# Attention block of a gated cross-attention layer: products with V in two groups of eight heads instead of four groups of four

## What is computed

```
q, k, v = projections of layernorm(x), ctx, ctx;  per head h of 16 (D = 16)
attn = q k^T / sqrt(D)                     # [256, 256] per head
p    = softmax(attn)
out  = p v                                 # [256, 16] per head
x    = x + tanh(g) * (concat(out) Wo + bo)
```

## Time and profile before

| | us |
|---|---|
| median of 3 runs | 318.63 (318.26 to 318.68) |
| span of the profiled execution, first to last instruction | 315.9 |
| projections and what comes ahead of step 0 | 0 to 81 |
| attention steps 0 to 7 and their tail | 81 to 231 |
| feed-forward layer | 231 to 316 |
| PE busy over the span | 239.1 (76%) |
| DVE busy | 218.9 (69%) |
| ACT busy | 176.1 (56%) |

### The profile page before, as it was taken

The page is one execution under the profiler, slowest core; times in us unless marked ns, Lnnn a source line. Parts: engine busy times, 40 slices in busy tenths (PEclk is TensorE's granted clock), DMA queues, the critical chain, the costliest instruction groups (busy, mean ns, idle before and its releaser), DMA issues.

```text
span 315.9 us, 6549 instructions
## 1 busy us (share of the span) xinstructions
PE 239.1 (76%) x1781; PEld 159.2 (50%) x1785; DVE 218.9 (69%) x465; ACT 176.1 (56%) x327; POOL 124.5 (39%) x213
## 2 busy tenths in 40 slices
PE   1799897999543999999999999999610578823951
PEld 1678676777322575757565656556400233312630
DVE  2579787765611769696979798894144389975992
ACT  2327583666711676676767667678501478836920
POOL 3366655232113135353434444353022395410074
PEclk9999999999955999999999999999875599995895
DMA  7767999933303353535353544000000000000025
GB/s 240 192 163 238 340 259 258 233 101 102 100 0 84 75 116 80 112 84 115 73 115 70 117 81 101 1 1 2 3 3 0 0 2 0 0 0 0 3 95 172
DMA packets 29734, 29.45 MB, mean 93 GB/s; under 512 B 5136, under 2 KB 26384, under 8 KB 29712
## 3 DMA queue, kind: packets, MB, share of 16 engines
q1 hardware_dynamic: 26832, 27.87, 34.8%
q10 hardware_dynamic: 2880, 1.31, 1.6%
HBM read 20.65 MB, written 8.39 MB: 92 GB/s over the span
## 4 chain that ended last, share of the span: by engine, by line
PE 27%; issue 14%; DVE 13%; POOL 6%; ACT 5%; DVEq 1%; DMA 1%; POOLq 0%; ACTq 0%; SPq 0%
PE bank_o L1281 6%; PE bank_a L1264 6%; PE bank_m L1307 5%; PE bank_b L1251 5%; DVE neg_max L801 3%; POOL x_rows L562 2%; PE bank_m L1289 2%; POOL arena L541 2%; PE bank_m L1297 2%; DVE x_rows L900 1%; ACT wgu_rows L761 1%; POOL big L553 1%; DVE arena L1076 1%; ACT big L662 1%; DVE stats L908 1%
## 5 line engine op out<-in xcount | busy, mean ns | idle before, releaser
L801 DVE TENSOR_REDUCE neg_max<-bank_b 128x2 f32<-128x512 f32 x112 | 73.9, 679 | 24.3 <-PE bank_b L1251 24.3
L662 ACT ACTIVATE big<-bank_a 128x512 f32<-128x512 f32 x128 | 69.8, 589 | 27.3 <-PE bank_a L1264 26.8
L1264 PE MATMUL bank_a<-big 98*128 98x256 bf16 x256 | 49.9, 278 | 9.5 <-DMA big<-max_parts 7.9
L1251 PE MATMUL bank_b<-big 96*128 96x256 bf16 x224 | 43.8, 277 | 0.0
L1281 PE MATMUL bank_o<-big,v_cur 128*32 128x256 f32 x512 | 35.8, 399 | 4.5 <-POOL v_cur L470 3.6
L1264 PEld LDWEIGHTS bank_a<-big 98*128 98x128 bf16 x256 | 21.4, 98 | 20.6 <-DMA big<-max_parts 8.4
L1173 PE MATMUL bank_a<-arena,w_t 128*128 128x256 f32 x128 | 31.1, 393 | 0.5 <-DVE resid L812 0.5
L476 POOL CAST max_parts<-max_f 8x256 bf16<-8x256 f32 x16 | 6.5, 405 | 56.0 <-ACT max_f L620 50.3
L1414 PE MATMUL bank_b<-wd_t,arena 128*128 128x256 bf16 x96 | 16.1, 323 | 14.4 <-DVE arena L1082 14.2
L1173 PEld LDWEIGHTS bank_a<-arena,w_t 128*128 128x128 f32 x128 | 24.4, 198 | 4.2 <-DVE resid L812 1.0
L449 POOL TENSOR_TENSOR arena<-resid,arena 128x512 bf16<-128x512 f32 x16 | 18.4, 1159 | 18.3 <-ACT arena L601 18.3
(11 more groups left out here) (157 smaller groups left out, 473.0 us busy)
## 6 DMA issues: line engine op xcount, KB each, us to landing
qk_parts<-arena SPq DMA_DIRECT2D x8, 768.0 KB, 5.0
big<-qk_parts SPq DMA_DIRECT2D x32, 192.0 KB, 3.7
big<-qk_parts SPq DMA_DIRECT2D x32, 128.0 KB, 4.0
x_rows<-in_x SPq DMA_DIRECT2D x8, 256.0 KB, 5.4
big<-qk_parts SPq DMA_DIRECT2D x32, 64.0 KB, 4.0
out<-x_rows SPq DMA_DIRECT2D x8, 256.0 KB, 2.2
big<-in_ctx SPq DMA_DIRECT2D x7, 256.0 KB, 6.9
wd_rows<-in_L_ffn_w_down SPq DMA_DIRECT2D x1, 704.0 KB, 8.2
```

The source lines that it names most:

```text
L662: act.activation(p_buf[:, h % HH], bank_a[:, h % 2].rearrange("p (c s) -> p c s", c=QC), ACT.Exp, scale=SCALE).then_inc(exp_done, 1)
L801: dve.tensor_reduce(neg_max[:, p, :, h], bank.rearrange("p (c s) -> p c s", c=QC), axis=AX.X, op=ALU.max, negate=True).then_inc(max_done, 1)
L1251: done = mm(to, q_st[0:KR, p, h, c * P:(c + 1) * P], k_st[0:KR, p, h], start=True, stop=not masked)
L1264: done = mm(to, k_st[0:KM, p, h, k * P:(k + 1) * P], q_st[0:KM, p, h], start=True, stop=not masked)
```

## The change

The heads are taken in two groups of eight (`GH = 8`, `GROUPS = 2`). `pv` of a group is 16 matmuls that fill the whole of `bank_o`; `ot` copies 512 columns; `back` is four transposes into all of `bank_m`; `rec` and `div` take eight heads at once. `p_buf` no longer wraps: the probabilities of heads 8 to 11 go to `resid`, 12 to 15 to a free part of `arena`, so that all 16 are kept. `o_t` is one buffer of 512 columns instead of two of 256. The three tables are new.

```diff
-    GROUPS = H // 4
+    GH = 8
+    GROUPS = H // GH
...
-    PE_AT = {("pv", 3): H + 1, "max_tr": 1, ("back", 3): H + 3, ("pv", 0): 5, "att_tr": H + 5, "out": H + 7,
-             ("pv", 1): 9, "next_max_tr": 9, ("back", 0): 11, ("pv", 2): 13, ("back", 1): 13, ("back", 2): H}
+    PE_AT = {("pv", 1): H + 1, "max_tr": 1, ("back", 1): H + 3, "att_tr": H + 6, "out": H + 8, ("pv", 0): 9,
+             "next_max_tr": 10, ("back", 0): 12}
...
+        p_last = part(4 * QC * S).rearrange("p (h c s) -> p h c s", h=4, c=QC)
+        p_third = resid[:].rearrange("p a w n -> p (a w n)").rearrange("p (h c s) -> p h c s", h=4, c=QC)
+        def p_of(h):
+            return p_buf[:, h] if h < HH else p_third[:, h - HH] if h < HH + 4 else p_last[:, h - HH - 4]
...
-                if not (start and h < HH):
-                    act.wait_ge(pv_done, GROUPS * b + h // 4 - 1)
+                if not start:
+                    act.wait_ge(pv_done, GROUPS * (b - 1) + h // GH + 1)
+                elif h == HH:
+                    act.wait_ge(lo_done, 2 * B)
...
-                    act.wait_ge(ot_tr, GROUPS * b + g - 1)
-                act.activation(o_t[:, g % 2], bank_o[:, 0:S], ACT.Copy).then_inc(ot_done, 1)
+                    act.wait_ge(ot_tr, GROUPS * b + g)
+                act.activation(o_t, bank_o[:], ACT.Copy).then_inc(ot_done, 1)
...
-                    pe.wait_ge(exp_done, H * b + 4 * g + 4)
+                    pe.wait_ge(exp_done, H * b + GH * (g + 1))
...
-                    for k in range(QC):
-                        for n in range(4):
-                            h = 4 * g + n
-                            done = mm(bank_o[n * 2 * D:(n + 1) * 2 * D, 0:S], v_cur[:, p, k, h],
-                                      p_buf[:, h % HH, k], start=(k == 0), stop=(k == QC - 1))
+                    for q in range(2):
+                        for k in range(QC):
+                            for n in range(4):
+                                h = GH * g + 4 * q + n
+                                done = mm(bank_o[n * 2 * D:(n + 1) * 2 * D, q * S:(q + 1) * S], v_cur[:, p, k, h],
+                                          p_of(h)[:, k], start=(k == 0), stop=(k == QC - 1))
...
-                        done = tr(bank_m[:, c * P:(c + 1) * P], o_t[:, g % 2, c * P:(c + 1) * P], ident_f[:])
+                        for q in range(2):
+                            done = tr(bank_m[:, (2 * c + q) * P:(2 * c + q + 1) * P],
+                                      o_t[:, q * S + c * P:q * S + (c + 1) * P], ident_f[:])
```

More of the change, by code:

```diff
@@ L90, in flamingo_block @@
     CT = CW // P
-    PE_AT = {("pv", 3): H + 1, "max_tr": 1, ("back", 3): H + 3, ("pv", 0): 5, "att_tr": H + 5, "out": H + 7,
-             ("pv", 1): 9, "next_max_tr": 9, ("back", 0): 11, ("pv", 2): 13, ("back", 1): 13, ("back", 2): H}
-    DVE_AT = {("rec", 0): 12, ("div", 0): 13, ("rec", 1): 14, ("div", 1): 14, ("rec", 2): H, ("div", 2): H + 1,
-              ("div", 3): H + 5, ("rec", 3): H + 4, "residual": H + 8, ("stats", 0): H + 10, ("stats", 1): H + 11,
-              "means": H + 12, "row_max": H + 15}
-    ACT_AT = {("ot", 3): H + 1, "max": 1, ("ot", 0): 7, "att": H + 5, ("ot", 1): 11, "next_max": 9, ("ot", 2): 13}
+    PE_AT = {("pv", 1): H + 1, "max_tr": 1, ("back", 1): H + 3, "att_tr": H + 6, "out": H + 8, ("pv", 0): 9,
+             "next_max_tr": 10, ("back", 0): 12}
+    DVE_AT = {("rec", 1): H + 4, ("div", 1): H + 5, "residual": H + 9, ("stats", 0): H + 11, ("stats", 1): H + 12,
+              "means": H + 13, ("rec", 0): 13, ("div", 0): 14, "row_max": H + 15}
+    ACT_AT = {("ot", 1): H + 1, "max": 1, "att": H + 6, "next_max": 10, ("ot", 0): 10}
     POOL_CHUNKS, DVE_CHUNKS = (1, 4), (0, 2, 3, 5)
@@ L147, in flamingo_block @@
         max_parts = sb("max_parts", [HH, 2, 2, S], BF16)
-        rec = sb("rec", [P, 2, QC, 4])
+        rec = sb("rec", [P, GROUPS, QC, GH])
         stats1 = sb("stats1", [P, 2, QC, 6])
@@ L200, in flamingo_block @@
         resid = sb("resid", [P, 2, 2, EC * S])
-        o_t = part(2 * S, True).rearrange("p (a s) -> p a s", a=2)
+        o_t = part(2 * S, True)
         att = part(2 * QC * E).rearrange("p (a c e) -> p a c e", a=2, c=QC)
@@ L659, in exp @@
                 act.wait_ge(s_done, H * b + h + 1)
-                if not (start and h < HH):
-                    act.wait_ge(pv_done, GROUPS * b + h // 4 - 1)
-                act.activation(p_buf[:, h % HH], bank_a[:, h % 2].rearrange("p (c s) -> p c s", c=QC), ACT.Exp,
+                if not start:
+                    act.wait_ge(pv_done, GROUPS * (b - 1) + h // GH + 1)
+                elif h == HH:
+                    act.wait_ge(lo_done, 2 * B)
+                act.activation(p_of(h), bank_a[:, h % 2].rearrange("p (c s) -> p c s", c=QC), ACT.Exp,
                                scale=SCALE).then_inc(exp_done, 1)
@@ L701, in other @@
                 else:
-                    ot_copy(b, what[1], start and what[1] < 2)
+                    ot_copy(b, what[1], start and what[1] == 0)
             def step(b, p, i=None, first=False, ahead=True):
@@ L716, in _ @@
                 other(what, 7)
-                if what == ("ot", 3):
+                if what == ("ot", 1):
                     ffn_weights(8)
@@ L878, in _ @@
             project(7, 1, 3, xs=False, st=False, heads=range(12, 16))
-            rows = bank_m[:, 0:QC * P].rearrange("p (c h x) -> p c h x", c=QC, h=4)
+            rows = bank_m[:].rearrange("p (c h x) -> p c h x", c=QC, h=GH)
             def reciprocals(b, g):
                 dve.wait_ge(ot_tr, GROUPS * b + g + 1)
-                chain.then(dve.reciprocal(rec[:, g % 2], rows[:, :, :, D]))
+                chain.then(dve.reciprocal(rec[:, g], rows[:, :, :, D]))
             def divide(b, p, g):
                 chain.wait()
-                dve.tensor_tensor(att[:, p, :, 4 * D * g:4 * D * (g + 1)].rearrange("p c (h d) -> p c h d", h=4),
+                dve.tensor_tensor(att[:, p, :, GH * D * g:GH * D * (g + 1)].rearrange("p c (h d) -> p c h d", h=GH),
                                   rows[:, :, :, 0:D],
-                                  rec[:, g % 2].unsqueeze(3).to_broadcast([P, QC, 4, D]), ALU.mult
+                                  rec[:, g].unsqueeze(3).to_broadcast([P, QC, GH, D]), ALU.mult
                                   ).then_inc(nrm_done, 1)
@@ L975, in _ @@
             with dve.Fori(0, 3) as i:
-                chain.loop(i, 12)
+                chain.loop(i, 8)
                 step(i * 2 + 1, 1)
@@ L1352, in attend @@
                     used = other(what, 7, 1, used)
-                    if what == ("back", 3):
+                    if what == ("back", 1):
                         ffn_weights(8)
```

## The result

| | before | after |
|---|---|---|
| median of the runs, us | 318.63 (5 runs, 318.26 to 318.90) | 331.17 (5 runs, 329.49 to 335.59) |
| the profiled execution, us | (no time of its own) | 334.24 |
| its span, us | 315.9 | 332.3 |

The changed kernel is slower: ratio 1.040, 95% interval 1.033 to 1.047. The profiled execution of after is a long one; three others have spans of 327.4, 327.8 and 329.1. So the profiles differ by 16.4 and the medians by 12.5. The ratios of the experiments are to executions of before made beside them, with medians of 317.60 to 317.75.

A forecast was written before the change was run, and what follows sets the result against it. PE sets the period, and the change spends the relays' margins, so PE waits for maxima at heads 0 and 8. Terms 2.9 + 8.7 + 0.5 + 3.1 + 1.6 = 16.8 lift the span to 332.7, time 335.4 us, range 323 to 343.

The forecast's parts named there:

- The relay: From next_max_tr through ACT's copy, POOL, SP and two DMAs to head 0's scores: 4.72 us, binding after the change.
- margin at head 0: In the kernel before, the first relay is through 0.5 us before head 0 starts.
- The waits: PE waits for the relays in each loop step: 1.19 us at head 0 and 0.64 at head 8.
- The step: One loop step, between scores that follow out: 17.94 us against 16.20, +8.7 over five periods.
- the second relay: From max_tr to head 8's scores: before 1.9 us to spare, after through at 15.62, a 0.64 wait.
- Step 0 and its start: First attention step, up to zero of step 1: 119.85 instead of 116.98, +2.9 us.
- the stream up to there is the same: Step 0's reason for pricing the second half of pv 0 at 1.00, after a first half of 1.80 at low clock.
- The last step: Final attention step: starts +0.5 us later, then +3.1 up to the second weights piece behind pv 0.
- The tail: End after the last pv: the wider last group costs +1.6 us in pv, ot, back, rec and div.
- Relay hidden: Rival: the relay doesn't bind, step 16.1, time 321 us (319 to 325); chance 0.12.
- Fewer instructions pay: Rival: PE waits for DVE to free bank_m, so 0.66 a step of rec and div is saved; 315.6 us, chance 0.10.
- The clock falls: Rival: the wait at head 0 lowers PE's clock in each of six steps, 9.4 us more, 345; chance 0.08.

The follow-up runs named there:

- e4: Kernel before plus an idle POOL memset of 8 x 1024 ahead of each cast of maxima; 319.65 us, 1.006 of before.
- e3: Changed kernel, own tables, with SP issuing the first row's DMA right behind POOL's cast instead of after the subtraction; 323.48 us, 1.016 of before.
- e8: Changed kernel with DVE's rounding of feed-forward weights moved from the last step to head 8 of step 0; 332.96 us, 1.044 of before.
- e5: Kernel before with the feed-forward weights rounded in step 0 instead of the last step; 317.72 us, 1.000 of before.
- e6: Kernel before with weights rounded in step 0 and the first row's DMA issued early; 317.32 us, 0.998 of before.
- e9: Changed kernel with e1, e2 and e3 together, weights rounded in step 0, and stats and means earlier on DVE; 322.19 us, 1.014 of before.
- e11: e9 with the rounding of the weights left in the last step; 322.98 us, 1.017 of before.
- e13: e11 with next_max_tr, pv 0, back 0 and the ACT copies for them one head later; 317.86 us, 1.001 of before.
- e1: Changed kernel with next_max_tr ahead of pv 0, both behind head 10; 326.50 us, 1.028 of before.
- e2: e1 plus ACT's copy of the maxima taken ahead of ot 1; 325.36 us, 1.022 of before.

## Why the prediction came out, point by point

The forecast, 335.4 with 323 to 343, was 4.2 above the median, and 1.2 above the profiled execution against which the sum was made. Its cause was right: the relay binds, at the two places named. Its terms were less good than their sum. Between the profiles the forecast has 2.9 + 8.7 + 0.5 + 3.1 + 1.6 = 16.8 and the measurement 6.2 + 6.3 + 3.9 + 0.1 = 16.4, the last step being 3.9 against 3.6. That these sums agree to 0.4 is luck: step 0 and the last step were forecast 3.6 too cheap, the loop and the tail 3.9 too dear.

**The relay**, predicted as 0.50 + 0.54 + 1.16 + 2.52 = 4.72, is 0.50 + 0.56 + 1.14 + 2.49 = 4.69. The waits, predicted as 1.19 and 0.64, are 1.27 (from 129.42, when in a full stream head 0 would follow the pair of head 15) and 0.62; the idle times in brackets, 1.11 and 0.46, count from the end of the matmuls ahead. The relay and its margin at head 0 were rightly read from the kernel before: e4 shows the margin there, and e3 that after has none.

**The step**, predicted as 17.94, is 17.37 to 17.59, 17.45 on the mean; the term that failed is the price of `pv`. A group of four was taken as 1.00 (16 products, in the chain of before too), so eight as 2.00; 32 products take 1.86 there. Twice a step that is 0.28. Another 0.13 is in the second relay (4.81 from `max_tr` to head 8 against 4.94) and 0.14 in `out`, for which the earlier trace rows gave 1.88 and whose scores follow at 1.73. Together that is a step of 17.4, which three of the five are; the other two are about 0.2 longer, and why isn't settled. Five periods cost 6.3 instead of 8.7.

**Step 0 and its start**, predicted as +2.9, came to +6.2 (123.16 against 116.98), for three reasons, none of them in the sum: 1.0, 0.85 and 1.9, of which smaller terms give 0.4 back. Head 8 of step 0 started 1.0 later. The whole of `pv 0`, not half of it, ran at the low clock:

```profile
100.86 0.61 PE L1272 MATMUL bank_a<-big 98*128 98x256 bf16 x2 [13.20 <-DMA big<-max_parts]
...
102.68 3.60 PE L1290 MATMUL bank_o<-big,v_cur 128*32 128x256 f32 x32
```

against 2.75 predicted. The step that failed is the one from "the stream up to there is the same" to a second half at full clock. Three windows from the scores of head 8 to the end of the low clock, in before, after and e4 (groups of four):

```profile
99.83:103.17 3.34, 3.34 (x24) 1.61 (x24) 1.39 (x2) 1.20 (x2) 0.00 (x0) 0.50 1.03 220
100.86:106.10 5.24, 5.24 (x40) 2.43 (x40) 1.39 (x2) 1.19 (x2) 0.00 (x0) 0.50 0.70 149
99.82:105.40 5.58, 5.58 (x34) 2.92 (x35) 1.80 (x3) 2.16 (x4) 0.75 (x1) 0.50 0.68 140
```

The wait ahead was 7.9, 13.2 and 8.5, so its length alone doesn't decide how long the low clock lasts: e4, with the stream of before, has it as long as after. Before's 3.3 is the shortest of all fourteen profiles, and the forecast took it as a property of the stream.

And one landing took twice its time, as the chain has it:

```profile
117.23 3.63 DMA big<-max_parts
```

It isn't chance: in e8, the other kernel with the same tables, the same landing takes 3.53 (at 119.36), and all others that ended a wait take 1.75 or 1.76, in every profile. In both kernels one packet of instructions (0.02 MB, queue q8) is fetched in these 2.5 us, and the copy that SP issues next but one takes 1.05 or 0.89 instead of 0.42. The trace's packet records settle that the data was late. The two rows go as 16 packets of 512 bytes; 15 have started by 118.56, and the last starts at 119.50, when the packet of instructions (118.48, 1.04 long) ends, and its semaphore update comes at 120.86. In e8 the last starts at 121.56, the end of the instruction packet (120.60, 0.96 long), and the others by 120.70. So one packet stood behind the fetch; why its update took 1.36 more isn't settled. What made the profiled execution longer than three others isn't either. The start varies too: in the kernels with groups of eight head 8 of step 0 begins anywhere from 97.35 to 103.24.

**The last step**, +0.5 and +3.1, came to +3.9 (27.99 against 24.09 from the scores to the last `pv`): near, by two errors that cancel. Head 8 came 7.77 behind head 0 where 8.6 was forecast: the forecast took the 3.24 of before's last step from `max_tr` to SP, in which POOL was slow beside the rounding (2.20 in the loop), and after took 2.89. But `out` behind the wait ran at the low clock, 3.31 for 1.88.

**The tail**, predicted as +1.6 for the wider group, is -0.1 from the last `pv` to the residual (7.70 against 7.82). The width does cost nearly that much: in e4, e5 and e6, where nothing in the tail is cold, the same stretch takes 6.21 or 6.22, so 1.5 less than in after. What was left out is that in the profile of before the last `out` was itself cold. In before and in after:

```profile
226.19:229.77 3.58, 3.58 (x8) 2.50 (x8) 0.00 (x0) 1.36 (x2) 0.00 (x0) 0.54 0.02 5
```

```profile
244.04:246.01 1.97, 1.97 (x8) 1.41 (x8) 0.00 (x0) 1.36 (x2) 0.00 (x0) 1.00 0.03 8
```

A granted clock of 0.54 against 1.00 for the same eight products: 1.6.

**The rivals.** *Relay hidden* is refuted for the change. Where e9 and e11 hide it, the step is 16.4 and not the 16.1 that was worked out; but they do so in another order, in which `next_max_tr` waits behind the residual, a wait that the sum for the change's own order had no term for. In the change's own order the relay was never hidden in full (e3 still waits 0.51 at head 0, with a step of 16.37), so the 16.1 itself wasn't tried. *Fewer instructions pay*: DVE's 0.40 a step is off the path, as forecast. Yet the e13 kernel's 15.88 shows that the groups of eight, well ordered, do run a step in 0.3 less; the two `pv` are 2 x (2.00 - 1.86) = 0.28 shorter than four and save two gaps of 0.09, which is enough for it, but this wasn't tried alone. `div` of 256 elements took 0.413, against 0.42 forecast and 0.57 for two of 128. The advice of the Trainium skill to take wide tiles ("VectorE: DVE Perf Modes", section "The TRN2 errata — SBUF-src ops pay a fixed extra latency per instruction") is given for operations that read SBUF; the trace shows one wide operation cheaper than two narrow ones for `div`, which reads `bank_m` in PSUM, too. It weighs nothing where DVE waits for PE.

*The clock falls*, as a price of every step, did not happen: waits of 1.11 and 0.46 in a step leave the granted clock at 1.00 in all windows. In the last step, where the wait for the second relay grew to between 1.1 and 3.6, `out` took 3.04 to 3.62 (after, e1, e2, e3, e8), and in e9, e11 and e13, where the wait ahead was none, 0.56 and 0.81, it took 1.97, 1.89 and 1.89. So the warning of the Trainium skill ("TensorE: Matmul & The Clock Gate", section "HAM oscillation — how this bites in real kernels") found its place in the last step, behind the wait for the DMA, at 1.2 to 1.7 in these five profiles, and not in the loop.

## What to carry to other kernels

Before moving a producer behind wider work, follow it through every engine to its consumer and compare the length of that relay with the distance that is left: here 4.7 us in five small steps (ACT's copy, POOL's cast and subtraction, SP's issue, the landing), with 0.5 to spare, decided a change that left PE's work untouched. A bound that is removed uncovers the next one, so count the waits behind it also in the order that the edit makes (the reader of a shared bank here). A wait is only free cover for work that the awaited engine doesn't feel. And one profile of before is one execution: a clock that came back early and a cold matmul at its end were read here as properties of the kernel.

## What the runs showed of the hardware that was not expected

Beside DVE's first pass over the weights (f32 to bf16) small operations on POOL (128x2) went from 0.20 to 1.32 and 0.86, a copy of 128x512 from 0.67 to 1.46 and an all-reduce from 0.40 to 2.46; beside the second pass (bf16 to bf16) the cast of 8x256 went from 0.39 to 1.01. It goes both ways: a piece of the second pass took 2.41 in after, beside POOL's subtraction and an addition, and 0.47 in e8. Beside DVE's reductions from PSUM, in the loop, the small operations have their short times. The Trainium skill, "GPSIMD Engine Reference", section "1. Specifications", has GpSimd's SBUF interfaces shared with VectorE and names contention with certain VectorE instructions; the trace agrees in that each slow operation lies beside one of these passes.

A DMA of 4 KB landed in 1.75 or 1.76 whenever it was waited for, except at the one place beside a fetch of instructions (3.63 and 3.53). There one of 16 packets started 1.0 late, when a 16 KB packet of instructions ended. And 32 products in a row took 1.86 in the chain where 16 took 1.00, so that the time of a short group must not be doubled: by these two numbers an estimated 0.14 is paid once a group.
